# The last pair of experts added by one-hot products, the shared rows added on VectorE or TensorE, the last batch scaled by VectorE

## The reference

```python
x = _layernorm(x + _L1_ffn_ref(x, ...), axis=-1)
# in _L1_ffn_ref:
scores = softmax(x @ gate_w.T); topk_w, topk_i = top_k(scores, 6)      # 64 experts
buf[e, slot] = x[token]            # at most CAP = 32 tokens for an expert
y = einsum('eci,eih->ech', silu(buf @ w_gate) * (buf @ w_up), w_down)
out_slots = y[flat_i, slot] * (flat_w * valid)
return out_slots.sum over the 6 choices + silu(x @ sw_gate) * (x @ sw_up) @ sw_down   # shared rows
```

## Time and profile before

| | |
|---|---|
| median of three runs | 1477.53 us (1477.4 to 1481.35) |
| the profiled execution | 1473.92 us, its span 1472.1 us |
| share of the span busy: PE, VectorE, ScalarE, GpSimd | 95%, 64%, 39%, 38% |
| mean granted TensorE clock | 0.983 of full speed |

### The profile page before, as it was taken

How to read it: one execution, slowest core, us unless ns; L and a number is a source line. 1 busy time by engine, 2 the same in 40 slices (tenths; PEclk the granted TensorE clock), 3 DMA queues, 4 the chain that set the end, 5 groups by cost and what they waited for, 6 DMA issues and landing times.

```text
span 1472.1 us, 23873 instructions
## 1 busy us (share of the span) xinstructions
PE 1396.1 (95%) x8118; PEld 1114.2 (76%) x8118; DVE 934.9 (64%) x2158; ACT 579.7 (39%) x1459; POOL 555.5 (38%) x483
## 2 busy tenths in 40 slices
PE   8999999999999999999999999999999999998990
PEld 7777777777777777777777788888888888875650
DVE  5777777777877777874443457547647647885113
ACT  4444444444444444551221144334334333352322
POOL 3655555555555555400113023513423422204223
PEclk9999999999999999999999999999999999999986
DMA  5000000000002100020000020020020001479984
GB/s 182 1 11 1 12 0 11 0 11 0 11 0 63 11 0 0 14 62 11 1 0 0 1 80 8 12 76 8 9 78 7 7 15 40 126 254 311 277 235 128
DMA packets 68221, 76.39 MB, mean 52 GB/s; under 512 B 14205, under 2 KB 55445, under 8 KB 68149
## 3 DMA queue, kind: packets, MB, share of 16 engines
q1 hardware_dynamic: 56517, 58.36, 13.4%
q10 hardware_dynamic: 8560, 12.36, 2.7%
q0 software_dynamic: 3072, 4.72, 1.6%
HBM read 66.22 MB, written 9.21 MB: 51 GB/s over the span
## 4 chain that ended last, share of the span: by engine, by line
PE 81%; DVE 7%; POOL 4%; ACT 3%; issue 2%; DMA 2%; SPq 1%; POOLq 0%; ACTq 0%; DVEq 0%
PE ps L1699 37%; PE ps L1838 9%; PE ps L1812 7%; PE ps L1800 5%; PE ps L1875 4%; PE ps L1966 4%; PE ps L1805 2%; PE ps L2198 2%; PE ps L2049 2%; PE ps L2258 1%; DMA wo<-in_L_attn_wo_dram 1%; PE ps L2039 1%; PE ps L2275 1%; PE ps L1840 1%; PE ps L1802 1%
## 5 line engine op out<-in xcount | busy, mean ns | idle before, releaser
L808 ACT ACTIVATE probs<-ps,nm 128x128 f32<-128x128 f32 (+3 forms) x256 | 134.0, 526 | 150.1 <-DVE nm L1189 150.1
L650 POOL TENSOR_TENSOR qk<-q,ksb 128x512 f32<-128x512 f32 x64 | 83.5, 1304 | 285.4 <-ACT q L903 212.3
L1838 PE MATMUL ps<-kT,qT 128*128 128x128 f32 (+3 forms) x512 | 174.5, 449 | 4.4 <-ACT probs L808 4.4
L1104 DVE TENSOR_TENSOR pT_low<-ps,pT 128x384 fp32r<-128x384 f32 (+2 forms) x256 | 99.6, 451 | 123.1 <-ACT pT L734 121.9
L1121 DVE TENSOR_TENSOR prod<-ps,rope_sb 128x1024 f32<-128x1024 f32 x128 | 150.2, 1215 | 7.4 <-PE ps L1699 7.4
L734 ACT ACTIVATE pT<-ps 128x384 fp32r<-128x384 f32 (+2 forms) x256 | 84.7, 416 | 152.4 <-PE ps L1875 152.4
L524 POOL TENSOR_TENSOR qT<-prod 64x512 f32<-64x512 f32 x64 | 81.2, 1269 | 167.4 <-DVE prod L1121 128.8
L1812 PE MATMUL ps<-U,oT 128*128 (+1 forms) x512 | 124.5, 386 | 0.0
L524 POOL TENSOR_TENSOR kT<-prod 64x512 f32<-64x512 f32 x64 | 81.4, 1272 | 108.7 <-DVE prod L1121 106.2
L1189 DVE TENSOR_REDUCE nm<-ps 128x1 f32<-128x128 f32 (+3 forms) x256 | 113.6, 484 | 9.3 <-PE ps L1840 9.3
L1246 DVE SCALAR_TENSOR_TENSOR acc<-ps,rinv,acc 128x256 f32<-128x256 f32 x256 | 109.4, 478 | 11.9 <-PE ps L1812 11.9
(11 more groups left out here) (263 smaller groups left out, 2767.9 us busy)
## 6 DMA issues: line engine op xcount, KB each, us to landing
eg<-in_L_ffn_w_gate_dram SPq DMA_DIRECT2D x16, 704.0 KB
eg<-in_L_ffn_w_up_dram SPq DMA_DIRECT2D x16, 704.0 KB
ed<-in_L_ffn_w_down_dram ACTq DMA_DIRECT2D x10, 640.0 KB
ksb<-ks_dram SPq DMA_DIRECT2D x16, 256.0 KB, 3.3
ed<-in_L_ffn_w_down_dram SPq DMA_DIRECT2D x6, 640.0 KB
rows_dram<-rows ACTq DMA_DIRECT2D x4, 640.0 KB, 9.0
acc<-in_L_attn_x_dram SPq DMA_DIRECT2D x4, 512.0 KB
wq_in<-in_L_attn_wq_dram SPq DMA_DIRECT2D x8, 256.0 KB, 2.9
```

Source lines behind the costliest of these rows:

```text
L650: nc.gpsimd.tensor_tensor(qk[:], q3[:], ksb[b % 2][:], ALU.mult).then_inc(qk_ready, 1)
L808: nc.scalar.activation(probs[hh][:, off:off + (i + 1) * P], ps[:, BS + i % 2, 0:(i + 1) * P], ACT.Exp, bias=nm[:, hh, i:i + 1], accum_out= ...
L1104: return nc.vector.tensor_tensor(o, whole, hi.bitcast(F32), ALU.subtract)
L1838: pe.matmul(ps[:, bank, 0:(i + 1) * P], qT[:, hh, b, i * P:(i + 1) * P], kT[:, hh, b, 0:(i + 1) * P], start=True, stop=False)
```

## The change

It has four parts.

1. GpSimd scatters only groups 0 to 13 (`SCATTERED`), and SyncE loads the sums once these have landed. Groups 14 and 15 are added on chip: VectorE makes for each of the two groups a matrix `onehot[h]` of 128 slots x 2048 tokens that holds a 1 where the slot's token number is the column (two instructions of 1024 columns each, compared with a row of numbers `tokens` that GpSimd writes with an iota ahead of scatter 10). `last_rows(b)` on TensorE multiplies `onehot[h]` with `y_in[h]` for each tile of 128 tokens. So `sum_repeats(7)`, its copy and its two scatters are gone.
2. The shared rows: for batch 0 VectorE adds the products of part 1 onto the shared rows in `acc` (`first_sums`), and then those onto the loaded sums. For batch 1 TensorE writes the shared rows into the two PSUM banks first, as products with the unit matrix, in two pieces: one ahead of `down(15)`, one behind it. For batches 2 and 3 that product with the unit matrix stands in the chain of each tile. VectorE then adds each bank of PSUM (two tiles, 128x512) to the loaded sums (`add_sums`).
3. The shift of batch b-1 is made in the middle of the statistics of batch b.
4. The last batch is scaled by VectorE (`last_tiles`), not by ScalarE, and is stored in two halves.

The diff, cut to its core:

```diff
-            sp.wait_ge(scattered, 16 * GROUPS)
+            sp.wait_ge(scattered, 16 * SCATTERED)
...
-            for b in range(BATCH):
+            for b in range(BATCH - 1):
                 sp.wait_ge(out_done, TPB * b + TPB)
                 sp.dma_start(out_dram[b], ...)
+            for lo in (0, TPB // 2):
+                sp.wait_ge(last_done, last_done_first + lo + TPB // 2)
+                sp.dma_start(out_dram[BATCH - 1][:, lo:hi, :], ...)
...
-            for s in range(GROUPS):
+            for s in range(SCATTERED):
+                if s == 10:
+                    pool.wait_ge(gate4_ready, BATCH * FT1)
+                    nc.gpsimd.iota(tokens[:], pattern=[[1, TOK // 2]], ...).then_inc(consts4, 1)
...
-            summed_rows(GROUPS // 2 - 1)
+                if s == 12:
+                    dve.wait_ge(consts4, 10)
+                    dve.wait_ge(down4, 2 * BATCH)
+                    link(nc.vector.tensor_scalar(spare[:, 0:2], idxf[:, SCATTERED:GROUPS], float(-(TOK // 2)), None, ALU.add))
+                if s in (12, 13):
+                    h = s - 12
+                    settle()
+                    for half, index in enumerate((idxf[:, s + 2:s + 3], spare[:, h:h + 1])):
+                        nc.vector.tensor_scalar(onehot[h][:, half * (TOK // 2):(half + 1) * (TOK // 2)], tokens[:], index, None,
+                                                ALU.is_equal).then_inc(onehot_ready, 1)
+            def add_sums(b):
+                dve.wait_ge(sums_loaded[b], sums_loaded_first[b] + 16)
+                dve.wait_ge(y_summed, SCATTERED // 2 + b + 1)
+                for j, bank in enumerate(last_banks[b]):     # two banks for each batch
+                    t = b * TPB + 2 * j
+                    link(nc.vector.tensor_tensor(fin[:, t:t + 2, :], fin[:, t:t + 2, :], ps[:, bank, :]..., ALU.add))
+                settle()
...
+            def last_tiles():
+                b = BATCH - 1
+                dve.wait_ge(rstd_ready, 13 + b)
+                for t in range(b * TPB, b * TPB + TPB):
+                    nc.vector.tensor_scalar(fin[:, t, :], fin[:, t, :], meanvar16[:, t, 0:1], rstd16[:, t:t + 1],
+                                            ALU.subtract, ALU.mult).then_inc(last_done, 1)
+            first_sums()
+            add_first_sums()
+            statistics16(0, fin)
+            for b in range(1, BATCH):
+                add_sums(b)
+                statistics16(b, fin, lambda: last_shift(b - 1))
+            last_tiles()
...
+                if s == GROUPS - 1:
+                    pe.wait_ge(shared_done, 2 * BATCH)
+                    shared_of_second(1)
                 down(s)
...
-            sum_repeats(GROUPS // 2 - 1)
+            def last_rows(b):
+                if b == 0:
+                    pe.wait_ge(onehot_ready, onehot_first + 4)
+                    pe.wait_ge(y_scaled, GROUPS)
+                for i in range(TPB):
+                    o = ps[:, last_banks[b][i // 2], (i % 2) * D:(i % 2 + 1) * D]
+                    t = b * TPB + i
+                    if b >= 2:
+                        pe.matmul(o, ident[:], acc[:, t, :] if b < BATCH - 1 else shared_last[:, i, :], start=True, stop=False)
+                    for h in range(2):
+                        last = pe.matmul(o, onehot[h][:, t * P:(t + 1) * P], y_in[h][:], start=b == 0 and h == 0, stop=h == 1, ...)
+                last.then_inc(y_summed, 1)
+            shared_of_second(0)
+            for b in range(BATCH):
+                last_rows(b)
```

More of the change, by code:

```diff
@@ L210, in program @@
         shared_last = place("shared_last", 20, [P, TPB, D])
+        onehot = [place(f"onehot{h}", at, [P, TOK]) for h, at in enumerate((32, 76))]
+        tokens = place("tokens", 24, [P, TOK // 2])
         wtmp = place("wtmp", 19.25, [P, GROUPS, 4])
@@ L274, in program @@
         shift_ready = sem("shift_ready")
+        onehot_ready, onehot_first = gw_turned, 1
+        last_done, last_done_first = x3_ready, TILES
         wq3_loaded, wk3_loaded, wv3_loaded, wo3_loaded = (
@@ L1403, in add3, with statistics16 @@
                 nc.vector.tensor_tensor(a, a, ps[:, 6 + tile % 2, 0:D], ALU.add).then_inc(added3, 1)
-            def statistics16(b, source):
+            def statistics16(b, source, between=None):
                 for t in range(b * TPB, b * TPB + TPB):
+                    if between is not None and t == b * TPB + TPB // 2:
+                        between()
                     link(nc.vector.bn_stats(stat16[:, t, :], source[:, t, :]))
@@ L1669, in _ @@
                     hidden_rows(s + 2)
-            summed_rows(GROUPS // 2 - 1)
-            def last_statistics(b):
-                dve.wait_ge(sums_loaded[b], sums_loaded_first[b] + 16)
-                dve.wait_ge(shared_done, 2 * b + 2)
-                at = slice(b * TPB, b * TPB + TPB)
-                shared = acc[:, at, :] if b < BATCH - 1 else shared_last[:]
-                link(nc.vector.tensor_tensor(fin[:, at, :], fin[:, at, :], shared, ALU.add))
-                settle()
-                statistics16(b, fin)
@@ new lines, in add_sums, with first_sums @@
+            def add_sums(b):
+                dve.wait_ge(sums_loaded[b], sums_loaded_first[b] + 16)
+                dve.wait_ge(y_summed, SCATTERED // 2 + b + 1)
+                for j, bank in enumerate(last_banks[b]):
+                    t = b * TPB + 2 * j
+                    link(nc.vector.tensor_tensor(fin[:, t:t + 2, :], fin[:, t:t + 2, :],
+                                                 ps[:, bank, :].rearrange("p (i n) -> p i n", i=2), ALU.add))
+                settle()
+            def first_sums():
+                dve.wait_ge(y_summed, SCATTERED // 2 + 1)
+                for j, bank in enumerate(last_banks[0]):
+                    t = 2 * j
+                    link(nc.vector.tensor_tensor(acc[:, t:t + 2, :], acc[:, t:t + 2, :],
+                                                 ps[:, bank, :].rearrange("p (i n) -> p i n", i=2), ALU.add))
+                settle()
@@ L1682, in last_norm, with add_first_sums, last_shift @@
+            def add_first_sums():
+                dve.wait_ge(sums_loaded[0], sums_loaded_first[0] + 16)
+                link(nc.vector.tensor_tensor(fin[:, 0:TPB, :], fin[:, 0:TPB, :], acc[:, 0:TPB, :], ALU.add))
+                settle()
+            def last_shift(b):
                 dve.wait_ge(rstd_ready, 13 + b)
@@ L2297, in _, with shared_of_second @@
             gate_up(0)
+            def shared_of_second(j):
+                pe.wait_ge(hE_ready, GROUPS)
+                if j == 0:
+                    pe.wait_ge(hET_ready, GROUPS)
+                t = TPB + 2 * j
+                pe.matmul(ps[:, last_banks[1][j], :], ident[:], acc[:, t:t + 2, :].rearrange("p i n -> p (i n)"),
+                          start=True, stop=True, skip_group_check=True)
             for s in range(GROUPS):
@@ L2314, in _ @@
                     down4_products(3, s - 10)
-            sum_repeats(GROUPS // 2 - 1)
+            def last_rows(b):
+                if b == 0:
+                    pe.wait_ge(hid4_ready, BATCH * FT1)
+                if b == 2:
+                    pe.wait_ge(y_copied, SCATTERED // 2)
+                if b == 0:
+                    pe.wait_ge(onehot_ready, onehot_first + 4)
[6 more added lines that the diff above has]
+                    for h in range(2):
+                        last = pe.matmul(o, onehot[h][:, t * P:(t + 1) * P], y_in[h][:], start=b == 0 and h == 0, stop=h == 1,
+                                         skip_group_check=b == 1)
+                last.then_inc(y_summed, 1)
+            shared_of_second(0)
+            for b in range(BATCH):
+                last_rows(b)
 def rope_tables():
```

14 lines of the change are left out of this document (8 added, 6 removed).

## The result

| us | before | changed |
|---|---|---|
| median (lowest to highest), 5 runs each | 1479.11 (1477.4 to 1481.35) | 1470.66 (1469.26 to 1473.82) |
| ratio of the two, 95% interval | | 0.9946 (0.9935 to 0.9958) |
| the profiled execution, its span | 1473.92, 1472.1 | 1473.82, 1472.1 |

The interval is 6.2 to 9.6 us of 1479.11. The two spans are equal, but they can't be compared: the profiled execution of before is none of its five and was 3.5 us faster than the fastest of them, the one of the changed kernel is the slowest of its five. What can be compared is the last stretch. It begins where the same instruction starts in both kernels, VectorE's copy of pair 6 (1434.76 in the earlier trace rows), and ends with the span. I call it the tail: 1472.1 - 1434.76 = 37.34 before. Ahead of that copy the change adds little but the comparisons.

What follows compares the result with a forecast made beforehand. The closing chain of scatter rounds, load, VectorE, GpSimd, scaling and store bounds the end while TensorE idles: -6.37 + 0.67 + 0.24 + 0.17 - 1.68 + 0.05 = -6.9, so 1477.53 becomes 1470.6 us; range 1467.5 to 1475.5.

Steps and rivals of the forecast that it cites:

- The scatter round: Before the load of the sums: group 13's landing releases the load, one scatter round fewer; -6.37 us.
- The comparisons: VectorE's four 128x1024 one-hot comparisons, 1.22 us each, delay the copy of pair 6; +0.67 us.
- The products: TensorE's 40 products of 128x256 after down(15), 0.43 us each at granted clock 1.00, done ahead of VectorE's adds.
- Dear weights: Rival: each TensorE product pays for its weights, 0.63 us each; no change, 1477.6 us; chance 6%.
- the clock didn't fall: Rival that it falls during TensorE's products: 0.85 us each, span +9.1, 1486.6 us; chance 5%.
- The cover for the last batch: TensorE finishes batch 3's products 0.8 us before VectorE needs them; with cheap comparisons both arrive together.
- The rest of the adds: VectorE's batches 1 and 2: adds reading PSUM and the shift inside the statistics cost +0.24 us.
- The shift and the last scaling: End of GpSimd to last tile: four VectorE scalings, 1.37 us, replace 3.05, which included the wait behind batch 2; -1.68.
- The store of half the size: The last store has half the bytes; gain between nothing and half of 2.9 us, taken as nothing.
- GpSimd beside the comparisons: Rival: comparisons shut GpSimd out of group 11's descriptors; scatter up to 1.3 us later, at most 0.6 showing, inside the forecast (79%).

Runs made afterwards that it cites:

- Parts 1 and 2 alone: Changed kernel with ScalarE scaling the last batch, one store for it, and shifts behind the statistics as before; tail 31.45 us, ratio to before 0.9962.
- The seven forms: Changed kernel plus seven VectorE scaling or comparison forms (1024 or 256 columns), each timed three times behind the last scaling; each grows 0.40 us from 256 to 1024 columns.
- The kernel with the slower comparison: Changed kernel with its four comparisons written as two-operand instructions; 1.22 us each, 30.2 us from the end of pair 6's product to the end.
- four more products: Changed kernel with four extra 128x256 products on TensorE ahead of batch 0's, their result overwritten; tail 31.49 us, ratio to before 0.9963.
- the kernel without shared rows for batch 3: Changed kernel without TensorE's four unit-matrix products in batch 3, whose shared rows are left out of the sum; tail 29.55 us.
- the repeat: The changed kernel measured again with no edit; tail 29.71 us, ratio to before 0.995.
- the one with the gap: Changed kernel, but TensorE begins the 40 products only once batch 0's sums have landed; tail 40.0 us, ratio to before 1.0013.

## Why the prediction was right

The time came out at 1470.66 where 1470.6 was forecast. That the two agree to 0.06 is luck. The forecast was 1477.53 - 6.9; with two runs more the median of the kernel before is 1479.11, 1.58 higher, and the medians differ by 8.45, 1.55 more than forecast. What can be held against the working is the tail.

The steps from the copy of pair 6 to the end, in us. "Forecast" is the tail by the prediction's terms, 37.34 - 6.92. It counts from the point where the copy could start without the comparisons; in the changed kernel that is also where it did start, 0.02 behind its product.

| step | forecast | measured |
|---|---|---|
| comparisons ahead of the copy, then copy to issue of the load | 0.67 + 6.59 | 6.56 |
| load to VectorE's batch 0 | 3.90 | 3.92 |
| batch 0 to the add of batch 3 | 9.95 | 10.12 |
| add of batch 3 to the last variance | 3.45 | 3.42 |
| GpSimd | 1.12 | 1.12 |
| four scalings | 1.37 | 1.38 |
| to the end of the span | 3.37 | 3.21 |
| sum | 30.42 | 29.73 |

- **The scatter round** (-6.37) went as forecast: one landing releases the load, and nothing that took its place is as long. From the copy to the issue of the load it is 6.56 instead of 1447.70 - 1434.76 = 12.94, so -6.38. Parts 1 and 2 alone measured -5.89: there this step is 6.70, so -6.24; 0.06 comes back at the load (3.96 instead of 3.90), and 0.29 between batch 0 and the last variance, for the adds through PSUM and a short wait for TensorE.
- **The comparisons** (+0.67) is the mis-sized term: they cost nothing. The step that failed is "four in 1.37 is one column a clock". I divided the duration of a short instruction by its columns, and took its fixed time for a rate. The seven forms show both apart: 0.52 ns a column and 0.28 fixed at two such operands. The end that I hadn't taken, 0.69 from the copy, was nearly right: 0.75. The kernel with the slower comparison shows the mechanism itself: at 1.22 each the copy is late by 0.54. So the mechanism held, and the price was that of another instruction.
- **The products** at 0.43 each and a clock of 1.00: 17.43 measured for 40, 17.4 forecast. Dear weights didn't occur, and the clock didn't fall. The cover for the last batch was given as 0.8, or none if the comparisons are cheap. They are, and VectorE waited 0.19 for them; four more products showed in full (1.76).
- **The rest of the adds** (+0.24 for batches 1 and 2) came out at +0.13: without a wait for TensorE it is 9.84 from batch 0 to the add of batch 3 (the kernel without shared rows for batch 3), and before it was 9.71. TensorE's 0.28, which the sum didn't have, makes it 10.12; so two misses partly cancel.
- **The shift and the last scaling** (-1.68, with 0.02 of gaps): from the end of GpSimd to the last tile it is 1.41 instead of 3.05, so -1.64. The experiments give 0.74 + 0.98 = 1.72 on top of parts 1 and 2: that is the 1.64 and the store's 0.16, less 0.08 for the shift inside batch 3's statistics. What the prediction didn't see is that this holds only because part 2 has changed the adds: without it the two give 1.05, since `rstd` takes 1.92.
- **The store of half the size** was given nothing; the last one landed 2.8 behind its issue instead of 2.9, and 0.16 is what the last step gained.
- **GpSimd beside the comparisons**: GpSimd's timeline of the changed kernel has the scatter of group 11, beside which the comparisons run:

```profile
1437.24 1.66 POOL L740 DMA_INDIRECT sums_dram<-xg,sidx  x1 [0.30 <-issue]
```

Undisturbed it takes 1.55, so it is 0.11 longer here (2.01 in the repeat, 1.74 with four more products, and 1.56 with the two-operand comparison), while one comparison took 0.92 instead of 0.75. Nothing of it reached the tail of the changed kernel. GpSimd shut out for up to 1.3, as the rival supposed, didn't show in any kernel; the most is 0.46. But the landing of this scatter can be late by more than that: 3.9 behind its start here and 4.0 before, 4.8 in the repeat, 4.9 in the kernel without shared rows for batch 3 and 5.3 in the one with the gap. In the last two it held the next pair, by 0.08 and by 0.9, and 0.9 is more than the 0.6 that the prediction allowed this rival. GpSimd took 1.72 in both, so most of the delay isn't its; where it comes from the runs leave open.

In sum, the tail is 0.69 shorter than forecast, 0.67 of it one term; the rest are misses of under 0.3 that cancel. The tail's 7.61 lies inside the 6.2 to 9.6 of the interval, and nothing measured calls for an effect outside it.

## What to carry to other kernels

When a chain of small transfers ends a kernel and the matrix engine idles beside it, do the last of them as a product with 0/1 matrices: one scatter round here was worth 6.4 us, and 40 products beside it cost 0.3. Price an instruction from two rows of different length, never from one duration divided by its columns. When moving an operation earlier, ask what the engine that feeds it is held by: `rstd` and the shift were free beside adds that read PSUM, and cost 0.7 beside adds of two SBUF tiles.

## What was not expected of the hardware

- A VectorE instruction with an operand of one value for each partition costs a fixed 0.06 us for each such operand, at 256 and at 1024 columns alike, beside 0.52 ns a column.
- VectorE and GpSimd hold each other in both directions. VectorE's add of two SBUF tiles makes GpSimd's 128x4 `rstd` 1.92 to 1.99 instead of 1.01; GpSimd's add of 128x1024 makes VectorE's 128x4 `shift` 2.26 instead of 0.15.
- The clock's return doesn't follow from the length of the gap. In the kernel with the gap, 8.2 us without products, the level was 0.50 from about 1446.4 to 1456.6, so for the last 3.7 us of that with products. In the kernel before, with the 3.3 us gap of the earlier trace rows, it was 0.50 from about 1405.1 to 1415.4, although TensorE was busy without a pause from 1406.3 on: 9.1 us. What decides it, the runs leave open.
